# Store waits moved from the end of the first block to batch 5 of the second, and the statistics of one group moved ahead of the quotients of batch 2

## The reference

```python
xn = layernorm(x)                                   # per row, eps 1e-5
Q, K, V = relu(xn @ Wq + bq), relu(xn @ Wk + bk), relu(xn @ Wv + bv)   # 16 heads of 8
s = layernorm(causal_softmax(Q K^T / sqrt(8)) @ V + xn) * gamma + beta  # rows whose sum is 0 are masked
f = layernorm(xn) * ln_scale + ln_bias
f = f @ attn_w.T + attn_b + xn
e = gelu(f @ w1[e] + b1[e]) @ w2[e] + b2[e]         # 8 experts, each for fixed 256-row slices
g = silu(gelu(e @ next_w.T + next_b))
out = x + s * g
```

## Time and profile before

| | kernel before |
|---|---|
| median of three runs | 457.64 us (457.45 to 457.67) |
| profiled execution, its own time | 456.26 us |
| its span, first to last instruction | 454.5 us |
| mean granted TensorE clock | 0.941 |
| PE busy | 382.5 us (84%) |
| DVE busy | 373.8 us (82%) |
| ACT busy | 289.8 us (64%) |
| POOL busy | 202.4 us (45%) |

### The profile page before, as it was taken

The page is one execution under the profiler, slowest core; times in us unless marked ns, Lnnn a source line. Parts: engine busy times, 40 slices in busy tenths (PEclk is TensorE's granted clock), DMA queues, the critical chain, the costliest instruction groups (busy, mean ns, idle before and its releaser), DMA issues.

```text
span 454.5 us, 9696 instructions
## 1 busy us (share of the span) xinstructions
PE 382.5 (84%) x3495; PEld 252.4 (56%) x3495; DVE 373.8 (82%) x876; ACT 289.8 (64%) x580; POOL 202.4 (45%) x522
## 2 busy tenths in 40 slices
PE   0056999799499977999999999999999999999850
PEld 0013777577377754566656656665666566566420
DVE  5989979799798215778999899998999998989427
ACT  0004788488389840267877877877778778778740
POOL 8532316625632012101236547456556383565591
PEclk9999999699699995579999999999999999999995
DMA  8920030673525658023232332423432414240000
GB/s 216 333 59 1 1 99 1 154 151 90 141 72 137 163 144 141 4 56 94 74 96 72 90 102 81 110 69 99 98 93 65 127 57 122 70 110 27 4 24 24
DMA packets 32198, 41.72 MB, mean 92 GB/s; under 512 B 5926, under 2 KB 24726, under 8 KB 32150
## 3 DMA queue, kind: packets, MB, share of 16 engines
q1 hardware_dynamic: 31990, 41.08, 35.2%
q0 software_dynamic: 160, 0.03, 0.0%
HBM read 26.43 MB, written 11.02 MB: 82 GB/s over the span
## 4 chain that ended last, share of the span: by engine, by line
PE 49%; DVE 10%; issue 2%; ACT 1%; POOL 0%; DVEq 0%; ACTq 0%; POOLq 0%
PE banks L1221 15%; PE banks L1184 9%; PE banks L1204 9%; PE banks L1186 6%; PE banks L1206 5%; DVE mx L1020 5%; PE banks L1293 2%; DVE stats L1065 2%; PE banks L1231 2%; DVE res L1059 1%; ACT pt L1139 1%; PE banks L1193 0%; DVE res L1046 0%; DVE res L1049 0%; DVE mixed L1050 0%
## 5 line engine op out<-in xcount | busy, mean ns | idle before, releaser
L1020 DVE TENSOR_REDUCE mx<-banks 128x1 f32<-128x512 f32 (+3 forms) x352 | 202.8, 634 | 27.9 <-PE banks L1186 25.9
L1139 ACT ACTIVATE pt<-banks 128x512 f32<-128x512 f32 x320 | 169.8, 601 | 47.8 <-PE banks L1206 40.2
L1221 PE MATMUL banks<-pt,vg 128*18 128x512 f32 (+3 forms) x1024 | 81.7, 437 | 0.7 <-ACT pt L1139 0.7
L911 POOL TENSOR_SCALAR mneg<-mx 128x16 f32<-128x16 f32 x32 | 8.1, 253 | 117.9 <-DVE mx L1020 116.7
L1184 PE MATMUL banks<-k_own,q_own 76*128 76x384 bf16 (+2 forms) x192 | 53.2, 301 | 6.6 <-DVEq L1097 4.1
L1184 PE MATMUL banks<-w_room 76*128 76x384 bf16 (+2 forms) x192 | 48.1, 274 | 3.3 <-DVE mx L1020 3.3
L1204 PE MATMUL banks<-q_own,k_own 76*128 76x384 bf16 (+2 forms) x192 | 49.4, 283 | 0.0
L1204 PE MATMUL banks<-w_room 76*128 76x384 bf16 (+2 forms) x192 | 47.5, 275 | 0.9 <-ACT pt L1139 0.5
L1221 PEld LDWEIGHTS banks<-pt,vg 128*18 128x18 f32 x1024 | 23.7, 97 | 44.2 <-issue 33.7
L1186 PE MATMUL banks<-k_own,q_own 124*128 124x128 bf16 x256 | 47.7, 235 | 0.0
L1186 PE MATMUL banks<-w_room 124*128 124x128 bf16 x256 | 43.8, 219 | 0.0
(11 more groups left out here) (198 smaller groups left out, 768.1 us busy)
## 6 DMA issues: line engine op xcount, KB each, us to landing
k_scratch<-parts SPq DMA_DIRECT2D x40, 128.0 KB, 2.4
k_own<-k_scratch SPq DMA_DIRECT2D x48, 96.0 KB
w_room<-k_scratch SPq DMA_DIRECT2D x48, 96.0 KB
q_scratch<-parts SPq DMA_DIRECT2D x24, 128.0 KB, 2.4
q_own<-q_scratch SPq DMA_DIRECT2D x32, 96.0 KB
w_room<-q_scratch SPq DMA_DIRECT2D x32, 96.0 KB
w_room<-in_w_dram SPq DMA_DIRECT2D x1, 2048.0 KB, 11.6
q_own<-q_scratch SPq DMA_DIRECT2D x16, 112.0 KB
```

Source lines behind the costliest of these rows:

```text
L1020: dve.tensor_reduce(mx[:, u % 2, heads[0]:heads[-1] + 1, q], banks[:, S0 + slots[0] % SLOTS, 0:w * len(heads)].rearrange("p (h k) -> p h k ...
L1139: act.activation(pt[:, T * j:T * j + T], banks[:, bank(), :], ACT.Exp, scale=SCALE).then_inc(exp_done, 1)
L1221: ins = mm(banks[32 * h:32 * h + VP, OT, P * k:T], vg[:, g, k, h, :], pt[:, KPLACE[k, h]:KPLACE[k, h] + n], start=(k == 0 and g % 2 == 0), ...
```

## The change

Three places. The four waits of SP for the last stores leave the end of the first block and stand at the start of batch 5 (`B - 3`) of the second block, ahead of the maxima and the loads of batch 6. On DVE the statistics of the second group stand after the rests of batch 1, ahead of the quotients of batch 2, and no longer after those of batch 2; the wait for the third load of x goes with them. On POOL `first_roots` of that group moves from behind the totals of batch 2 to behind those of batch 1, and `root_halves` from batch 3 to batch 2. The third group stays where it was (batches 4 and 5), written out by number. The tile `parts` is laid out behind `mask_b` and `maskT`, at the end of the first block's room.

```diff
--- before.py
+++ after.py
@@ -213,9 +213,9 @@
         eoT = s1("eoT", [P, T])
         full = s1("full", [P, 2, T])
         rest = s1("rest", [P, 2, T])
-        parts = s1("parts", [P, 2, 2, PARTS, T], BF16)
         mask_b = s1("mask_b", [P, NT], BF16)
         maskT = s1("maskT", [NT, P], BF16)
+        parts = s1("parts", [P, 2, 2, PARTS, T], BF16)
 
         TRX, TRL, QB, KB, VB, XB, H0B = range(7)
 
@@ -281,9 +281,6 @@
                         load_keys(sp, 0, 0, i - 2)
                 sp.wait_ge(w2_done, B)
                 load_fixed(sp, 1)
-                for o in range(2):
-                    for s in range(2):
-                        sp.wait_ge(parts_out[s][o], 16 * STORES[o] * (B // 2 + 1))
 
             @block.gpsimd
             def _(pool):
@@ -409,10 +406,14 @@
                     if i in FIRST:
                         second_roots(tok, GROUPS[FIRST[i]])
                     totals(tok, i)
-                    if i + 1 in FIRST:
-                        root_halves(GROUPS[FIRST[i + 1]])
-                    if i + 2 in FIRST:
-                        first_roots(tok, GROUPS[FIRST[i + 2]])
+                    if i == 2:
+                        root_halves(GROUPS[1])
+                    if i == 5:
+                        root_halves(GROUPS[2])
+                    if i == 1:
+                        first_roots(tok, GROUPS[1])
+                    if i == 4:
+                        first_roots(tok, GROUPS[2])
                 pool.wait_ge(maskT_ready, 1)
                 pool.dma_start(mask_dram, maskT[:, :]).then_inc(mask_out, 16)
                 pool.wait_ge(mask_out, 16)
@@ -568,10 +569,11 @@
                         lows(tok, i - 2)
                     if i > 0:
                         rests(tok, i - 1)
-                    if i + 2 in FIRST:
-                        if i == 2:
-                            dve.wait_ge(x_in[2], 16)
-                        statistics(GROUPS[FIRST[i + 2]])
+                    if i == 1:
+                        dve.wait_ge(x_in[2], 16)
+                        statistics(GROUPS[1])
+                    if i == 4:
+                        statistics(GROUPS[2])
                 masks()
                 lows(tok, B - 2)
                 rests(tok, B - 1)
@@ -866,6 +868,10 @@
 
                 def batch(tok, b):
                     par, last = b % 2, b == B - 1
+                    if b == B - 3:
+                        for s in range(2):
+                            for o in range(2):
+                                sp.wait_ge(parts_out[s][o], 16 * STORES[o] * (B // 2 + 1))
                     for g in range(NG):
                         if g < NG - 1:
                             maxima(tok, par, g + 1)
```

## The result

The changed kernel takes 451.6 us, the median of four runs (450.99 to 452.99); the kernel before ran beside it at 457.65. The ratio is 0.9878 (95% interval 0.9846 to 0.991). With the runs of the experiments added, the changed kernel has a mean of 452.7 us over 15 runs (standard error 0.24) and the kernel before 457.5 over 110 (0.12): a gain of 4.7 us, where the sum said 3.75. The two profiled executions differ by only 3.27 us (456.26 and 452.99).

The account below looks back on a forecast made before the run. The first block's end was taken to hang on DVE, which serves all batches in fixed order, the second block on PE; 3.69 us (statistics earlier) + 0.06 (waits) = 3.75 off 457.64 gave 453.9 us, range 452.2 to 456.2.

Parts of the forecast that it names:

- the sum: Whole kernel: 3.69 us from the earlier statistics plus 0.06 from the moved waits, a gain of 3.75 us.
- DVE's sum of 3.69 us: First block, DVE: quotients of batch 4 start 3.69 us earlier, 1.99 from the stall and 1.70 from the roots.
- POOL and the new gap: First block, batch 2: moved roots hold POOL 9.72 us ahead of the totals, giving PE a new 2.9 us gap.
- this gap would leave the clock up: PE at batch 2: no clock fall in the 2.9 us gap; the rival, a fall giving 454.6 us, had chance 0.22.
- Who waits next: First block after the move: splits have 2.0 us cover at batch 3; SP's long store issue may grow up to 1.7 us.
- The four waits: SP's waits for the last stores, moved to the second block: 0.06 us saved, at most 0.1 and at least nothing.
- The sum carried over to the median: Timed median stands 1.38 us above the profiled execution; difference carried over, so 457.64 - 3.75 = 453.9 us.
- the 1.99 us of those waits: DVE, 47 to 86 us: net waiting of 1.99 us for batches 0 and 1, gone once statistics come earlier.
- The range: Time of the changed kernel: 452.2 to 456.2 us with the rivals, leaving about 0.15 outside.
- a shorter stretch at the seam: Start of second block: rival that PE's half-clock stretch ends some 3 us sooner, 452.3 us, chance 0.07.
- the main case: The forecast of 453.9 us without the rivals, own range 453.2 to 454.8, chance 0.60.
- The value products: Second block, PE: the 27 us half-clock stretch was said to have ended once these products started.

Follow-up runs that it names:

- e9: Kernel before with idle PE products in the gaps of batch 0, ahead of batches 3 and 5, and 28 (not 10) at the first block's end: 447.94 us.
- e10: Changed kernel with idle PE products in the gaps of batch 0, ahead of batches 2 and 5, and 28 at the first block's end: 444.50 us.
- e6: Changed kernel with 4 instead of 22 idle PE products at the start of the first block: 452.06 us, ratio 0.9879 to the kernel before.
- e8: Changed kernel with 15 idle products added in PE's short gaps of batch 0: 453.33 us, ratio 0.9906 to the kernel before.
- e16: Changed kernel run again unchanged, the third time: 452.64 us, ratio 0.9886 to the kernel before.
- e18: Repeat of e14, the changed kernel with 28 instead of 10 idle products at the first block's end: 443.96 us, ratio 0.9718.
- e1: Changed kernel with the four store waits put back at the first block's end, so only statistics and roots move: 452.44 us, ratio 0.9883.
- e4: Changed kernel run again unchanged: 453.68 us, ratio 0.9906 to the kernel before.
- e14: Changed kernel with only the idle PE products at the first block's end raised from 10 to 28: 444.05 us, ratio 0.9692.
- e2: Kernel before with only the four store waits moved and the tile parts laid out last, statistics unmoved: 458.13 us, ratio 1.0003.
- e3: Kernel before run again unchanged, for its scatter and a second trace: 457.59 us, ratio 1.0004.
- e15: Kernel before run once more unchanged, for a third trace: 457.06 us, ratio 0.9995.
- e11: e9 with 15 more idle products (3.24 us of PE) ahead of the projections of batch 1, making PE late: 451.92 us, ratio 0.988.
- e7: Kernel before with 15 idle products added in PE's short gaps of batch 0: 456.55 us, ratio 0.9981.
- e13: Kernel before with only the idle PE products at the first block's end raised from 10 to 28: 446.85 us, ratio 0.9769.
- e17: Repeat of e13, the kernel before with 28 instead of 10 idle products at the first block's end: 446.78 us, ratio 0.9795.
- e5: Kernel before with 4 instead of 22 idle PE products at the start of the first block: 456.83 us, ratio 0.9986.

## Why the prediction was wrong

By its own steps:

- **DVE's sum of 3.69 us**: right. The rows add up to 3.66 (80.31 + 1.77 is 82.08 and not 82.05), and from the first quotients to those of batch 5 the two traces take 77.94 and 74.28 us: 3.66. Every start was forecast within 0.1 us. The second block is 3.53 us earlier and not 3.8, mainly because SP's last broadcast was issued in 1.99 us and not in 1.73; over all traces it takes 1.73 to 1.99 in either order, so that is scatter. e9 and e10 agree with the sum in time, to half a microsecond.
- **POOL and the new gap**: right, 3.23 for 2.9 us. That this gap would leave the clock up was wrong: wherever it had about its forecast length the clock fell (first, e6, e8 and e16, gaps of 3.09 to 3.25 us), and in e18 even at 1.93. Unfilled, the gap left it up only in e1, e4 and e14, where PE came late and the gap was 1.76 to 1.78. The fall cost DVE about 0.1 us or nothing, and 1.3 in e8.
- **Who waits next**: right. SP's long issue grew as described, and a store late by that delayed nobody:

```profile
91.63 5.10 SPq L272 DMA_DIRECT2D q_scratch<-parts  x3
```

  (3.70 in the earlier trace rows.)
- **The four waits**: taken as 0.06, measured as nothing (e2), since the drain behind them grows by 0.33.
- **The sum carried over to the median**: this is the step that failed. I added the 1.38 us between the profiled execution and the timed median to both kernels alike, as if it were an overhead of the launch. It was not: the mean of the kernel before stands 1.2 us above its first profiled execution, that of the changed kernel 0.25 us below its own. Such differences are scatter between executions, of which one profile shows one case. Some of it falls on both orders: the first quotients start between 27.9 and 29.0 us (28.23 in that profile, 28.82 and 29.01 in e3 and e15), and the second block is 280.4 to 282.0 us long. Some of it only the order before pays: PE's lateness after an early fall of the clock, passed on by DVE's waits at batch 2. The profile had no such fall. The sum removed the 1.99 us of those waits that this execution showed, and not what they become when PE is late: by the same reckoning 73.42 - 48.07 - 20.43 = 4.9 us in e2 and 73.19 - 47.54 - 20.43 = 5.2 in e11. The changed kernel's order covers them. That this cost exists is shown by e2 and e11, and e7 puts its size in the timed runs at about 1.0 us. That it is the whole surplus is not shown, and e13, e14, e17 and e18 speak against it: they have the same early gaps, and the two orders are only 3.4 us apart there.
- **The range**: its lower end had only a shorter stretch at the seam in it. Chance has a part in the miss: the mean over 15 runs, 452.7, would have been inside the range, though not inside the 453.2 to 454.8 of the main case; the first four runs, 451.8 in the mean, were 1.3 us below the eleven later ones.

## What to carry to other kernels

A stall by which one engine waits for another can be worth more than the profile shows, where the releasing engine's own speed varies between executions: ask not only how long the wait is, but what it becomes if the releaser is 3 us late, and whether the new order still waits at all. A block boundary that leaves PE idle for some microseconds deserves a look of its own at the granted clock behind it; 18 small products ahead of the barrier were worth 10.2 us in the order before and 8.9 in the new one, twice the change under study. And a difference between a profiled execution and a timed median is a quantity to explain before it is carried over.

## What was not expected of the hardware

- After the idle 4.1 to 4.4 us at the seam PE ran at 1.2 GHz for 23.9 to 27.3 us in every trace without the filler, although from its first matmul there it was busy nearly all of that time (26.2 of 27.0 us in the first trace, 27.2 of 27.4 in the changed kernel's, 23.8 of 23.8 in e4). In the first block, after gaps of 1.9 to 6.8 us, it was back at 2.4 GHz 3.4 to 6.8 us after the fall (10.2 once, in e5). What sets the difference (the kind of products or their size) was not tried. The value products, by which the prediction explained the end of the stretch, don't end it: in seven traces (e1, e2, e4, e5, e6, e8, e16) the clock is back 0.3 to 1.2 us before the first of them.
- The clock needs no long gap to fall: in e2 and e4 it fell behind gaps of 0.7, 1.4 and 1.2 us (ahead of the q projection, of L702 and of the product with attn_w) within 7 us, while in the first traces of both kernels the same gaps left it up. Nor is a long gap enough: 3.3 us ahead of batch 3 brought it down in most traces of the order before and left it up in e2 and e17.
- The drain of SP's queue took 377 ns where the last instructions before it were DMA issues, and 48 ns where four passed waits stood between.
